# Results of the first expert layer go home slot by slot, and the second layer's fronts start three slots earlier

## The reference

```
xn = layernorm(x)
layer 0: s = scan over the tokens: h = a*h + sigmoid(g)*tanh(v), a = 0.001 + 0.998*sigmoid(d)
         f = top-1 of 4 groups of 2 experts each: sum_e w_e * (silu(xn Wg_e) * (xn Wu_e)) Wd_e
xn = layernorm(x)
layer 1: s = causal linear attention in chunks of 128 (4 chunks a sequence, state carried), out projection
         f = shared expert + top-2 of 8 routed experts, each silu(. W1) * (. W3), then W2
```

## Time and profile before

| what | value |
|---|---|
| time, median of 3 runs | 413.4 us (409.56 to 415.67) |
| span of the profiled execution | 394.6 us |
| around the span (413.4 − 394.6) | 18.8 us |
| PE busy | 376.7 us (95%) |
| DVE, ACT, POOL busy | 267.8, 224.7, 217.3 us |
| mean granted TensorE clock | 0.980 |

### The profile page before, as it was taken

The page is one execution under the profiler, slowest core; times in us unless marked ns, Lnnn a source line. Parts: engine busy times, 40 slices in busy tenths (PEclk is TensorE's granted clock), DMA queues, the critical chain, the costliest instruction groups (busy, mean ns, idle before and its releaser), DMA issues.

```text
span 394.6 us, 6221 instructions
## 1 busy us (share of the span) xinstructions
PE 376.7 (95%) x1853; PEld 278.1 (70%) x1853; DVE 267.8 (68%) x744; ACT 224.7 (57%) x447; POOL 217.3 (55%) x211
## 2 busy tenths in 40 slices
PE   7979898999999998999999999999999999999995
PEld 5665346889898886866677667677676676676772
DVE  5987976434343565269699599598697696766573
ACT  3675985454545567688574664664644835823321
POOL 4437787730015150156948949849768678267352
PEclk9877999999999999999999999999999999999998
DMA  7996311510031000090600600701601601404100
GB/s 230 265 360 262 103 47 49 156 42 2 2 114 48 2 20 8 27 315 2 241 1 0 264 6 0 269 0 32 240 0 36 234 0 66 177 0 170 73 27 27
DMA packets 26590, 38.63 MB, mean 98 GB/s; under 512 B 2496, under 2 KB 22848, under 8 KB 24128
## 3 DMA queue, kind: packets, MB, share of 16 engines
q1 hardware_dynamic: 24512, 34.03, 25.6%
q0 software_dynamic: 2048, 4.23, 3.4%
HBM read 29.20 MB, written 9.05 MB: 97 GB/s over the span
## 4 chain that ended last, share of the span: by engine, by line
PE 70%; DVE 16%; ACT 7%; issue 4%; DMA 1%; POOL 0%; POOLq 0%; DVEq 0%; ACTq 0%
PE ps L960 11%; PE ps L851 7%; PE ps L951 6%; PE ps L949 6%; PE ps L950 6%; PE ps L831 4%; PE ps L833 4%; PE ps L832 4%; PE ps L861 4%; PE ps L935 3%; PE ps L772 2%; PE ps L888 2%; DVE score L1369 2%; DVE pr L1366 2%; PE ps L756 2%
## 5 line engine op out<-in xcount | busy, mean ns | idle before, releaser
L431 POOL TENSOR_TENSOR gu<-gu 128x512 f32<-128x512 f32 x64 | 84.3, 1324 | 61.9 <-DVE gu L1442 56.5
L949 PE MATMUL ps<-xc_round,w_round 128*128 128x512 f32 x144 | 82.9, 576 | 0.6 <-DVE gu L1430 0.5
L647 ACT ACTIVATE gu<-gu 128x512 f32<-128x512 f32 x64 | 40.3, 630 | 75.2 <-DVE gu L1442 75.1
L960 PE MATMUL ps<-gu,w2s 128*128 128x512 f32 x144 | 73.5, 593 | 0.5 <-POOL gu L431 0.5
L951 PE MATMUL ps<-xc_round,w_rest 128*128 128x512 f32 x144 | 56.8, 395 | 0.0
L950 PE MATMUL ps<-xc_rest,w_round 128*128 128x512 f32 x144 | 56.7, 394 | 0.0
L1442 DVE TENSOR_TENSOR gu<-ps,w_raw 128x512 f32<-128x512 f32 x64 | 43.7, 687 | 19.0 <-PE ps L951 18.4
L398 POOL DMA_INDIRECT xnT<-sorted_y,slot x32 | 31.3, 980 | 42.0 <-DMA sorted_y<-sorted_sb 34.1
L1295 DVE TENSOR_TENSOR sx_rest<-ps,sx_round 128x128 fp32r<-128x128 f32 x35 | 10.2, 291 | 54.5 <-ACT sx_round L560 54.5
L569 ACT COPY h0T<-ps 128x512 f32<-128x512 f32 x35 | 20.6, 588 | 42.3 <-PE ps L861 42.3
L388 POOL DMA_INDIRECT sorted_rows<-sorted_sb,slot x32 | 34.5, 1079 | 15.6 <-issue 9.1
(11 more groups left out here) (194 smaller groups left out, 758.6 us busy)
## 6 DMA issues: line engine op xcount, KB each, us to landing
w_raw<-score_rows SPq DMA_DIRECT2D x8, 1024.0 KB, 5.8
sorted_sb<-score_rows SPq DMA_DIRECT2D x4, 1024.0 KB, 4.6
w0d<-score_rows SPq DMA_DIRECT2D x4, 1024.0 KB, 7.3
sorted_rows<-zero_rows SPq DMA_DIRECT2D x1, 2340.0 KB, 15.5
xa<-in_x SPq DMA_DIRECT2D x8, 256.0 KB, 4.7
w_raw<-in_gate_up SPq DMA_DIRECT2D x1, 2048.0 KB, 12.9
out_x<-xa SPq DMA_DIRECT2D x7, 256.0 KB, 2.4
sorted_sb<-sorted_rows SPq DMA_DIRECT2D x1, 1690.0 KB, 8.0
```

The costliest lines, as they stand in the source:

```text
L431: pool.tensor_tensor(gu[:, e % RING, 1, :], gu[:, e % RING, 0, :], gu[:, e % RING, 1, :], ALU.mult).then_inc(s["m_h"], 1)
L647: nc.scalar.activation(gu[:, e % RING, 0, :], gu[:, e % RING, 0, :], ACT.Silu).then_inc(s["m_sg"], 1)
L949: pe.matmul(bank, w13_round[:, c], xc_round[par][:, :], start=True, stop=False)
L960: pe.matmul(ps[:, 3, :], w2s[:, w * P:(w + 1) * P], gu[:, e % RING, 1, :], start=(e == 0), stop=(e == E1)).then_inc(s["m_y"], 1)
```

## The change

Each row of tile t carries a 131st number, its home row in DRAM (ROW becomes 131; home row = 128*t + p + 1; 0 stands for an unused row). When a sorted tile has come in, DVE reads that column, replaces the zeros by rows in a spare area, and casts them to `home` (`homes_of`, once for tiles 0 to 8 and once for 9 to 34). After each slot POOL scatters the tile's result straight to `home_y` in DRAM by these numbers (`bring_home`). SP loads a sequence from `home_y` with one plain load (`load_y`): sequences 0 to 2 when the first 16 scatters have landed, 3 to 7 when all have. POOL's gathers are gone, in the slots and in layer 1. The splitting of w13 alternates with the first scatters (`SPLIT_AT = 2`). `T_GY` becomes (20, 24) and `T_TURN` 24.

```diff
-ROW = P + EPG
+ROW = P + EPG + 1
-T_GY = (23, 27)
-T_TURN = 27
+T_GY = (20, 24)
+T_TURN = 24
+SPLIT_AT = 2
...
-        sorted_y = nc.dram_tensor("sorted_y", [SORTED * P, P], F32, kind="Internal").ap()
+        home_y = nc.dram_tensor("home_y", [(TILES + SORTED) * P + 1, P], F32, kind="Internal").ap()
-        y_t = sorted_y.rearrange("(n p) c -> p n c", p=P)
+        y_t = home_y[1:TILES * P + 1].rearrange("(b t p) d -> b p t d", p=P, t=TPS)
...
-            def store_y(h):
-                sp.wait_ge(s["f_y"], Y_TILES[h + 1])
-                n = slice(Y_TILES[h], Y_TILES[h + 1])
-                sp.dma_start(y_t[:, n, :], sorted_sb[:, n, 0:P]).then_inc(y_stored[h], 16)
+            def load_y(b):
+                for h in range(part_of(b) + 1):
+                    sp.wait_ge(y_home[h], 16 * (Y_TILES[h + 1] - Y_TILES[h]))
+                sp.dma_start(seq_of(ya, b), y_t[b]).then_inc(gathered[b], 16)
...
-            store_y(0)
+            for b in range(PSEQ[0]):
+                load_y(b)
             store_scores(0)
-            sp.wait_ge(y_stored[0], 16)
             spread_scores(0, 0)
-            store_y(1)
             sp.wait_ge(s["f_down"], SORTED)
             spread_scores(0, 1)
+            load_y(PSEQ[0])
...
+                if j == 0:
+                    for b in range(PSEQ[0] + 1, SEQS):
+                        load_y(b)
...
-            def gather(b, part=slice(0, TPS)):
-                pool.wait_ge(y_stored[part_of(b)], 16)
-                for t in range(TPS * b + part.start, TPS * b + part.stop):
-                    pool.indirect_dma_start(
-                        ya[:, t, :], None, sorted_y[0:P * Y_TILES[part_of(b) + 1]],
-                        bass.IndirectOffsetOnAxis(ap=slot[:, t:t + 1], axis=0)).then_inc(gathered[b], 16)
+            def bring_home(n):
+                pool.wait_ge(s["homes"], 1 if n < FULL else PARTS)
+                pool.wait_ge(s["f_y"], n + 1)
+                pool.indirect_dma_start(
+                    home_y, bass.IndirectOffsetOnAxis(ap=home[:, n:n + 1], axis=0),
+                    sorted_sb[:, n, 0:P], None).then_inc(y_home[0 if n < Y_FIRST else 1], 16)
...
-            for p in range(PAIRS + 1):
-                split_w13(p)
-            gather(0)
-            gather(1)
-            scales(0)
-            rest_of(0)
-            gather(2)
-            scales(1)
+            for n in range(SORTED):
+                if n == T_GY[0] + 1:
+                    scales(0)
+                if n == T_TURN - 1:
+                    rest_of(0)
+                if n == T_GY[1] + 4:
+                    scales(1)
+                bring_home(n)
+                if SPLIT_AT <= n < SPLIT_AT + 2 * (PAIRS + 1):
+                    split_w13(n - SPLIT_AT)
...
-                if j < PSEQ[1]:
-                    gather(PSEQ[0] + j, slice(0, 2))
-                if j < PSEQ[1]:
-                    gather(PSEQ[0] + j, slice(2, 4))
...
+            def homes():
+                link(nc.vector.tensor_reduce(place_no[:, :], lower, AX_X, ALU.add))
+                link(nc.vector.tensor_scalar(place_no[:, :], place_no[:, :], -1.0, float(P), ALU.mult, ALU.add))
+                link(nc.vector.tensor_scalar(home_f[:, :], cst[:, C_TILE:C_TILE + SORTED], float(P), place_no[:, :],
+                                             ALU.mult, ALU.add))
+                nc.vector.tensor_copy(rows[:, :, P + EPG], home_f[:, 0:TILES])
+                nc.vector.tensor_scalar(away[:, :], home_f[:, :], float(TILES * P), None, ALU.add)
+
+            def homes_of(first, stop):
+                came = sorted_sb[:, first:stop, P + EPG]
+                to = home_f[:, first:stop]
+                link(nc.vector.scalar_tensor_tensor(to, came, 0.0, away[:, first:stop], ALU.is_equal, ALU.mult))
+                link(nc.vector.tensor_tensor(to, to, came, ALU.add))
+                nc.vector.tensor_copy(home[:, first:stop], to).then_inc(s["homes"], 1)
...
             groups(0)
             stats(7)
+            homes()
...
             rest_of_rows(0, 0)
+            homes_of(0, FULL)
             for n in range(SORTED):
                 if n == FULL:
                     dve.wait_ge(sorted_in[1], 16)
                 late_slot(n)
+                if n == FULL:
+                    homes_of(FULL, SORTED)
```

More of the change, by code:

```diff
@@ L135, in gated_recurrent_moe_two_layers @@
         slot = sb("slot", [P, TILES], U32)
+        home = sb("home", [P, SORTED], U32)
+        home_f = sb("home_f", [P, SORTED])
+        away = sb("away", [P, SORTED])
+        place_no = sb("place_no", [P, 1])
         group = sb("group", [1, SORTED], I32)
@@ L250, in gated_recurrent_moe_two_layers @@
             c_v c_lg c_lgm c_exp c_scores c_scoreT c_scoreT_out c_a c_at c_keys c_keys_out c_state c_state_out c_num c_s1
-            m_gu m_free m_sg m_h m_y m_gf m_gfT m_of m_xo score_stored""".split()
+            homes m_gu m_free m_sg m_h m_y m_gf m_gfT m_of m_xo score_stored""".split()
         s = {n: sem(n) for n in names}
@@ L254, in gated_recurrent_moe_two_layers @@
         sorted_in = [sem(f"sorted_in{h}") for h in range(PARTS)]
-        y_stored = [sem(f"y_stored{h}") for h in range(PARTS)]
+        y_home = [sem(f"y_home{h}") for h in range(PARTS)]
         spread_in = [sem(f"spread_in{i}") for i in range(2)]
@@ L358, in _ @@
             sp.wait_ge(o_stored, 16 * (SEQS + 1))
-            for h in range(PARTS):
-                sp.wait_ge(y_stored[h], 16)
         @block.gpsimd
@@ L393, in _, with split_w13 @@
             scatter(1)
-            def gather(b, part=slice(0, TPS)):
-                pool.wait_ge(y_stored[part_of(b)], 16)
-                for t in range(TPS * b + part.start, TPS * b + part.stop):
-                    pool.indirect_dma_start(
-                        ya[:, t, :], None, sorted_y[0:P * Y_TILES[part_of(b) + 1]],
-                        bass.IndirectOffsetOnAxis(ap=slot[:, t:t + 1], axis=0)).then_inc(gathered[b], 16)
-            def split_w13(p):
-                c = slice(4 * P * p, min(4 * P * (p + 1), W13S))
[L404 to L407, removed]
+            def bring_home(n):
[4 more added lines that the diff above has]
+                    sorted_sb[:, n, 0:P], None).then_inc(y_home[0 if n < Y_FIRST else 1], 16)
+            def split_w13(i):
+                p, rest = divmod(i, 2)
+                c = slice(4 * P * p, min(4 * P * (p + 1), W13S))
+                if rest:
+                    pool.wait_ge(s["w13_split"], 2 * p + 1)
+                    pool.tensor_tensor(w13_rest[:, c], w13_raw[:, c], w13_round[:, c].bitcast(F32),
+                                       ALU.subtract).then_inc(s["w13_split"], 1)
+                else:
+                    pool.tensor_copy(w13_round[:, c], w13_raw[:, c]).then_inc(s["w13_split"], 1)
             def scales(k):
@@ L586, in gy_silu @@
             def gy_silu(k):
-                act.wait_ge(gathered[k], 16 * TPS)
+                act.wait_ge(gathered[k], 16)
                 wait(act, "c_var", k)
@@ L1148, in weights_of_groups @@
                                              us.unsqueeze(3).broadcast_to([P, n, GROUPS, EPG]), ALU.mult))
-                nc.vector.tensor_reduce(rows[:, P0[h]:P0[h] + n, P:ROW], uw[:, 0:n, :, :].rearrange("p t g e -> p t e g"),
+                nc.vector.tensor_reduce(rows[:, P0[h]:P0[h] + n, P:P + EPG], uw[:, 0:n, :, :].rearrange("p t g e -> p t e g"),
                                         AX_X, ALU.add)
```

## The result

| kernel | median, us | range | runs |
|---|---|---|---|
| before | 413.21 | 409.56 to 415.67 | 4 |
| after | 407.74 | 406.83 to 408.02 | 4 |

The ratio is 0.9881 (95% interval 0.9836 to 0.9926): 5 us faster, inside the 2% called no change. Medians in this document are of all executions; ratios and their intervals leave out those more than 1.5% above the quickest of their kernel.

What follows compares the result with a forecast made beforehand. The prediction took a saturated TensorE as the bound, with 5.9 us idle from 80 us on. Its terms summed to nothing: span 394.6 + 0, with 18.8 us around it; forecast 413.2 us, range 409 to 417.

Steps and rivals of the forecast that it cites:

- part 1: Way home by scatters and plain loads: 25.2 us off POOL in layer two, gain 0; sequence 0 home 3.1 us early.
- rival C: Slower: POOL's descriptor work beside each slot holds up DVE, 0.3 us in 33 slots, 423 us; chance 0.04.
- 18.8 us lie around the span: Difference between the runs' median of 413.4 us and the traced span of 394.6 us, added to the predicted span.
- at most those 5.9 us: TensorE's idle time from 80 to 392 us, taken as the most the change could gain, 1.4% of the time.
- Rival A: Slower: y comes home late, ACT stands 2.9 us in slot 20 and PE nearly as long, 416.3 us; chance 0.12.
- Part 2: homes() adds about 1.1 us to DVE's prologue and homes_of little, hidden by idle time: cost 0, at most 1.6 + 0.6 us.
- rival D: homes() comes through with 1 to 2 us and the early front brings layer two no earlier, 415 us; chance 0.07.
- Part 3: Waits and queues: SP's loads and POOL's scales have cover, such as 15 us and 1.2 us; all cost 0.
- Part 4: Fronts three slots earlier: their collisions move along, slot 34's wait is replaced by one in slot 30; sum nothing.
- the 1.23 us stall of PE: Stall before 153.96 us, where ACT loads two activation tables around the softmax's exp; forecast to move three slots earlier.
- Rival B: Faster: collisions dissolve, most of 2.1 us from 127 to 172 and some of layer two's 3.8 go, 411 us; chance 0.15.

Runs made afterwards that it cites:

- x1: The kernel before, unchanged, measured again with its own trace: median 416.9 us, ratio to before 1.001.
- x4: The kernel before with the fronts three slots earlier and the old way home by gathers: median 412.2 us, ratio to before 0.9849.
- x7: The kernel before (old way home) with the 32 scatters of the way in replaced by two plain stores, rows left unsorted: median 400.9 us.
- x12: x7 repeated, unchanged, on the same chip as its version with spaced gathers: median 401.1 us, ratio to before 0.9736.
- x14: The kernel after, with POOL keeping at most two scatters of the way in in flight: median 409.2 us, ratio to before 0.9946.
- x9: x7 with its twelve gathers of the slots kept but issued one per slot instead of in runs: median 396.9 us.
- x13: x9 repeated, unchanged, on the same chip as x12: median 396.0 us, ratio to before 0.9616.
- x5: The kernel after (new way home) with the 32 scatters of the way in replaced by two plain stores, rows left unsorted: median 397.1 us.
- x8: x5 with the fronts put back late, to slots 23 and 27, and the turn to 27: median 396.8 us.
- x2: The kernel after, unchanged, measured again: median 417.6 us, ratio to before 0.9858.
- x10: x5 plus 14 spare scatters into rows nobody reads, POOL waiting for each to land before the next: median 408.3 us.
- x11: x5 plus 32 spare plain transfers of the same rows issued by SP, two in flight, into rows nobody reads: median 411.5 us.

## Why the prediction was wrong

The change gains because the runs of gathers, eight and then four in a row, are gone from layer one's slots. Five traces have the run of eight (before, x1, x4, x7, x12); four of them have a stand beside it, and in three (x1, x7, x12) PE waits 2.4 to 3.5 us for it and then has a stretch at half clock. Without it no trace has a stand in the slots but x14, whose first scatters home continue the row of the way in. The run of four has no stand beside it in any of the five; x9 and x13 took both runs apart, so the eight alone weren't tested. The size is shown where the way in is plain: 3.8 us for the change (x7 to x5) and 5.1 for taking the gathers apart (401.1 to 396.0), and x8 and x9 leave nothing for the fronts or for the scatter instead of the gather. For the complete kernels the first 5.5 us (ratio 0.988) fit it, and x1's trace has the stand; but beside each other on one chip x1 and x2 showed no gain in the median, so it is argued, not shown, that the 5.5 us are this gain and not partly luck of the batch.

Two steps of the prediction failed. The first is the "Gain 0" of part 1, for which it says "since PE waited for POOL once", and the reading behind it, "eight gathers lay in the slots without a trace on PE", which it held against rival C and never turned round. Both read a price that isn't paid in each execution from the single one that had been spared. In x1 the gathers stand beside 3.5 us of idle PE, and even there no wait names POOL: PE's is put down to ACT, and ACT's to nothing. So a table of waits for POOL couldn't price them. The second is "so 18.8 us lie around the span". That gap was the sign that the trace and the timed runs were different executions. Nothing in the trace could show where they went, but the argument "It can gain only where PE idles, at most those 5.9 us" rested on their not being there. In x1, a trace of the same kernel, the slots take 117.1 us in place of 102.5, most of it idle PE and half clock. That the measured 5.5 us lie under those 5.9 is chance: none of them came from the idle time that was counted. (The sum itself gives 413.4; the forecast says 413.2 without a reason for the 0.2.)

Point by point for the rest:

- Part 1, the trip home: 5.3 us were taken, 5.8 us measured (from the end of slot 15's copy at 121.70 to 127.5); y was 2.5 us early where 3.1 were forecast. Rival A did not come. The scatters home took 0.957 to 1.148 us, so the port that the Trainium skill ("SBUF — State Buffer", section "SBUF: two separate sides") has DVE and GpSimd share lengthened none by more than 0.19 us; it doesn't explain the stands: they are mostly ACT's, and that section has ACT's ports wait for nobody. POOL's time, 44.1 us forecast, is 34.2 us of busy time plus its issues, and it held up nobody. POOL's 20 us less in layer two were worth nothing, as forecast: 221.5 us before and 221.4 after, from slot 34's down to the last w2 matmul.
- Part 2, the addresses: hidden, as far as the traces can tell. The first down matmul is at 64.6 us in x8 and 66.7 in x5, both with homes(), and at 64.5 to 66.0 in the four without it (x7, x9, x12, x13), of which x7 and x12 are one kernel and still 1.3 us apart; `homes_of` has 0.16, 0.18 and 0.17 us at 62.3. Nothing speaks for rival D, and the time went the other way; a cost of a microsecond or so can't be excluded.
- Part 3, the queues: no wait of PE on POOL or DMA in the slots of after.
- Part 4: the 1.23 us stall of PE stands before 156.34 in after; it moved along with the front, as forecast, and the 45 us up to the same place in layer two hold 42.57 us of PE work in place of 42.91. Rival B, which came out nearest with 411, was right in its sign and wrong in its mechanism: nothing dissolved there or in layer two (216.05 us of PE work in place of 216.24).
- Rival C's mechanism, POOL's descriptor work against DVE: the slots are no longer with a scatter in each (x8 102.3 us, and 102.5 in x13, with its gathers in twelve of them).

What stays open: why ACT stands, and not ACT alone. DVE has waits that end "remote" too, 0.4 to 3.8 us, in seven of the traces that have stands and in none without. In x2 both end together, ACT's 3.85 us at 66.82 us and DVE's 3.83 us (the scan) at 66.92:

```profile
66.82 0.58 ACT L525 COPY sT<-ps 128x512 f32<-128x512 f32 x1 [3.85 <-remote]
66.92 1.22 DVE L1254 TENSOR_TENSOR_SCAN scan<-td,tg 128x512 f32<-128x512 f32 x1 [3.83 <-remote]
```

In the slots ACT's is the one that PE waits for. The transposes that it waits for are over, PE itself goes on with other work during the first microseconds, and the wait ends without an event that the trace has an instruction for. Whether the late thing is the signal or the engine these traces can't tell. That the stands need a close row of indirect transfers on POOL rests on 9 traces with such a row on the way in, of which 8 have stands there, and on 8 without, of which none has; the limit of distance between 1.26 and 2.5 us wasn't looked for. Nor was the length: beside the eight gathers ACT's first stand began 3.8 to 7.9 us after the first of them, and three or four in a row (the four gathers, the first three scatters home of after) made none.

## What to carry to other kernels

Hold the span of the profiled execution against its own timed run before taking a sum from it; here the two lay 2.0 us apart for one and the same execution, so a gap of 18.8 us meant that the trace was of another kind of execution, from which costs that fall at random were missing. Don't let GpSimd issue indirect transfers in a long row beside a TensorE pipeline that passes through ScalarE: one per slot cost nothing that shows here, a row of eight and one of four together 5 us, 32 in a row about 10 and most of the spread. When a few microseconds drown in noise, first take the source of the noise out of both kernels, even where that leaves a step of the computation out, and compare then; and price the waits that an experiment adds, as the 8 us of x10 and x11 show.

## What the runs showed of the hardware

- ScalarE stood idle for 0.2 to 12.5 us at a time before instructions whose release no record shows. All these waits began while GpSimd issued indirect transfers in a row, as a rule one every 1.25 to 1.27 us, or at most 0.2 us behind the last of them, and ended up to 3.0 us behind it. x2 has the longest, before 60.53 us, at least 10.1 us of it after TensorE's last matmul had ended (50.38 us); beside the gathers the copy came 3.2 to 4.0 us after the transposes that it needs (x1, x7, x12).
- VectorE has such waits in seven of the ten traces in which ScalarE has them, up to 3.8 us (x2).
- After an idle time of 3.5 us that a stand made, TensorE was granted half its clock, 1.2 GHz instead of 2.4: in x1 a clock of 0.50 from 136.3 to 142 us, and in x12, after 2.4 us of idle time, a mean of 0.98 over the slots against 1.00 in x13.
- 128 plain row transfers from SyncE's queue, 32 times, made no stand (x11).
